# GpSimd's two-operand tensor work moved to VectorE in a two-layer graph kernel

## The reference

```python
def conv(x, a, eps, W, b):            # layer 0, run for x and for x2 with the same adj
    ax = a @ x
    h = ax + (1 + eps) * ax
    for i in range(3):
        h = relu(h @ W[i].T + b[i])
    return h
merged = concat(conv(x, adj, eps1, W1, b1), conv(x2, adj, eps2, W2, b2)) @ Wm.T + bm
x = layernorm(x + merged)
A = adj + eye(4096); deg = A.sum(1); d = where(deg > 0, deg ** -0.5, 0)   # layer 1
x = layernorm(x + ((d[:, None] * A * d[None, :]) @ x) @ W.T + b)
```

## Time and profile before

| | |
|---|---|
| median of 3 runs | 649.18 us (649.15 to 649.63) |
| span of the profiled execution | 647.4 us |
| PE busy | 601.5 us, 93% |
| PEld busy | 485.3 us, 75% |
| DVE busy | 562.9 us, 87% |
| ACT busy | 364.9 us, 56% |
| POOL busy | 272.1 us, 42% |
| HBM read and written | 139.14 MB, 2.10 MB; 218 GB/s over the span |

### The profile page before, as it was taken

How to read it: one execution, slowest core, us unless ns; L and a number is a source line. 1 busy time by engine, 2 the same in 40 slices (tenths; PEclk the granted TensorE clock), 3 DMA queues, 4 the chain that set the end, 5 groups by cost and what they waited for, 6 DMA issues and landing times.

```text
span 647.4 us, 8346 instructions
## 1 busy us (share of the span) xinstructions
PE 601.5 (93%) x2692; PEld 485.3 (75%) x2692; DVE 562.9 (87%) x564; ACT 364.9 (56%) x441; POOL 272.1 (42%) x167
## 2 busy tenths in 40 slices
PE   5949999899999999999999999899989999999984
PEld 4738888678888878888878887557757878878863
DVE  5939998997999998899899799974799988988974
ACT  5514536562353773353675244175786787787772
POOL 0553606780340591160384159960465042340171
PEclk9969999999999999999999999999999999999998
DMA  8943753425536435336534473576588989999800
GB/s 298 413 177 121 269 195 131 175 91 190 189 137 240 149 130 194 130 130 230 183 141 159 162 292 125 199 281 237 196 296 328 359 338 402 344 353 376 320 33 34
DMA packets 21287, 141.54 MB, mean 219 GB/s; under 512 B 2320, under 2 KB 2832, under 8 KB 5008
## 3 DMA queue, kind: packets, MB, share of 16 engines
q1 hardware_dynamic: 20544, 139.15, 58.0%
q10 hardware_dynamic: 720, 2.10, 0.8%
HBM read 139.14 MB, written 2.10 MB: 218 GB/s over the span
## 4 chain that ended last, share of the span: by engine, by line
PE 27%; POOL 24%; issue 22%; DVE 21%; ACT 5%; DMA 1%; POOLq 0%; DVEq 0%; SPq 0%; ACTq 0%
PE ps L332 19%; DVE alo L625 13%; POOL hlo L774 6%; PE pd L350 3%; ACT ahi L482 3%; POOL rstd L790 3%; DVE rowsum L636 2%; POOL x1lo L860 2%; PE pd L362 2%; DVE rowsum L640 2%; POOL xb L780 2%; POOL xb L783 2%; POOL x1lo L822 2%; POOL yt L815 1%; POOL vareps L788 1%
## 5 line engine op out<-in xcount | busy, mean ns | idle before, releaser
L625 DVE TENSOR_TENSOR alo<-raw,ahi 128x1024 fp32r<-128x1024 f32 x255 | 356.0, 1414 | 61.3 <-ACT ahi L482 60.0
L482 ACT ACTIVATE ahi<-raw 128x1024 fp32r<-128x1024 f32 x255 | 267.6, 1059 | 248.1 <-PE ps L332 231.1
L332 PE MATMUL ps<-ahi,x1hi 128*128 128x512 f32 x504 | 163.7, 401 | 34.5 <-DVE alo L625 13.5
L332 PE MATMUL ps<-ahi,x2s 128*128 128x512 f32 x512 | 159.9, 391 | 0.0
L332 PE MATMUL ps<-alo,x1hi 128*128 128x512 f32 x504 | 158.9, 392 | 0.0
L332 PE MATMUL ps<-ahi,x1lo 128*128 128x512 f32 x504 | 158.7, 391 | 0.0
L332 PEld LDWEIGHTS ps<-ahi,x1hi 128*128 128x128 f32 x504 | 92.1, 189 | 66.4 <-issue 26.1
L332 PEld LDWEIGHTS ps<-ahi,x2s 128*128 128x128 f32 x512 | 97.0, 189 | 20.5
L332 PEld LDWEIGHTS ps<-ahi,x1lo 128*128 128x128 f32 x504 | 95.2, 189 | 20.3
L332 PEld LDWEIGHTS ps<-alo,x1hi 128*128 128x128 f32 x504 | 95.2, 189 | 19.9
L774 POOL TENSOR_TENSOR hlo<-h,hhi 128x512 fp32r<-128x512 f32 x36 | 79.2, 2233 | 68.8 <-ACT hhi L487 68.8
(11 more groups left out here) (66 smaller groups left out, 367.1 us busy)
## 6 DMA issues: line engine op xcount, KB each, us to landing
raw<-a_t SPq DMA_DIRECT2D x124, 1024.0 KB, 4.8
raw<-a_t SPq DMA_DIRECT2D x7, 512.0 KB, 8.8
xn<-x SPq DMA_DIRECT2D x3, 1024.0 KB, 8.6
out<-outn ACTq DMA_DIRECT2D x3, 512.0 KB, 5.4
par<-params SPq DMA_DIRECT2D x1, 708.0 KB, 14.2
xn<-x SPq DMA_DIRECT2D x2, 256.0 KB, 4.6
raw<-a_t SPq DMA_DIRECT2D x2, 256.0 KB, 5.1
xn<-x SPq DMA_DIRECT2D x1, 512.0 KB, 8.2
```

Of the source, the lines that this page charges most:

```text
L332: mm = pe.matmul(ps[bank][:, :], block_of(w, n), a[c], start=(n == 0 and k == 0), stop=(n == JB - 1 and k == 2))
L482: act.activation(ahi[:, n % SPLIT, :], raw_tile(layer, n), ACT.Copy).then_inc(hi_ready, 1)
L625: dve.tensor_tensor(alo[:, n % SPLIT, :], raw_tile(layer, n), as_f32(ahi[:, n % SPLIT, :]), ALU.subtract).then_inc(lo_ready, 1)
```

## The change

All of GpSimd's tensor work but the two powers (degrees to the -0.5, variance to the -0.5) goes to VectorE. It is written into VectorE's lists at fixed blocks:

- x pieces 3, 4, 5 are split at blocks 7, 12, 20 of the first quarter; `wlo` between the first and second quarter.
- `hlo` is split at blocks 3, 4 (two tiles each), 7 and 9 (four each) of the next quarter; the base at `DVE_BASE` and the block after.
- the variance plus epsilon stands behind the aggregation, the shift (now one instruction) two or three blocks later, behind a wait for GpSimd's power.
- y of quarters 0 to 2 is made at blocks 12, 20, 28 of the last layer-0 quarter and split two blocks later, that of quarter 3 at blocks 22 and 24 of the first layer-1 quarter. ACT rounds every y, at the block between, in one piece of 1024 (before: GpSimd for six of eight halves). TensorE waits for y once in 8 blocks, before once in 4. `xn` plus the bias is made in place, right behind each split.
- the identity goes into diagonal block n three blocks ahead (`AHEAD`).
- the normalisation of a layer-1 quarter starts on ACT at block 22, before 23.
- more quarters are written out in place of hardware loops on ACT and DVE.

```diff
-ACT_ROUND_Y = (23, 26)
+DVE_BASE = (10, 7)
+DVE_SHIFT = tuple(k + 2 for k in DVE_AGGREGATE)
+DVE_MAKE_Y = (KB + 4, 2 * KB + 4, 3 * KB + 4, 22)
+ACT_ROUND_Y = tuple(k + 1 for k in DVE_MAKE_Y)
+DVE_SPLIT_Y = tuple(k + 2 for k in DVE_MAKE_Y)
+AHEAD = 3
-ACT_NORM2 = DVE_AGGREGATE2 + 6
+DVE_SHIFT2 = DVE_AGGREGATE2 + 3
+ACT_NORM2 = DVE_SHIFT2 + 2
...
+            def round_y(g):                                   # ACT
+                act.wait_ge(yt_ready, g + 1)
+                act.wait_ge(block_used, (QUARTERS - 1) * JB + KB * (g + 1))
+                act.activation(x1hi[:, g, :], yt[:, :, :].rearrange("p k d -> p (k d)"),
+                               ACT.Copy).then_inc(yhi_ready, 1)
...
+            def split_h(q, l, m):                             # all from here: DVE
+                wait(dve, hhi_ready, q * (LAYERS * M) + (M * l + m + 1))
+                dve.tensor_tensor(hlo[:, m, :], h[:, m, :], as_f32(hhi[:, m, :]),
+                                  ALU.subtract).then_inc(hlo_ready, 1)
+            def variances(done, r=slice(0, KB)):
+                wait(dve, stats_ready, done)
+                dve.tensor_scalar(vareps[:, r], mv[:, r, 1], LN_EPS, None, ALU.add).then_inc(var_ready, 1)
+            def shifts(done, r=slice(0, KB)):
+                wait(dve, rstd_ready, done)
+                dve.scalar_tensor_tensor(out=nshift[:, r], in0=mv[:, r, 0], scalar=-1.0, in1=rstd[:, r],
+                                         op0=ALU.mult, op1=ALU.mult).then_inc(norm_ready, 1)
+            def mlp_step(q, n, plan):
+                if plan == 0:
+                    if n in (ACT_EVACUATE + 1, ACT_EVACUATE + 2):
+                        for m in range(CH):
+                            split_h(q, 0, CH * (n - ACT_EVACUATE - 1) + m)
+                    if n in ACT_RELU[0] and ACT_RELU[0][n] < LAYERS - 1:
+                        for m in range(M):
+                            split_h(q, ACT_RELU[0][n] + 1, m)
+                if n == DVE_BASE[plan]:
+                    residual_base(q)
+                if n == DVE_BASE[plan] + 1:
+                    residual_bias(q)
...
+                    variances(q + 1)
+                if n == DVE_SHIFT[plan]:
+                    shifts(q + 1)
+                    degree_factors(q)
+            def split_y(g):
+                dve.wait_ge(yhi_ready, g + 1)
+                dve.tensor_tensor(quarter(x1lo, g), yt[:, :, :], as_f32(quarter(x1hi, g)),
+                                  ALU.subtract).then_inc(y_ready, 1)
+                dve.tensor_tensor(quarter(xn, g), quarter(xn, g), bias_rows(BO_AT), ALU.add).then_inc(base_ready, 1)
+            def add_identity(q, n):
+                wait_raw1(dve, q, n)
+                k = n % KB
+                square = raw_tile(1, n)[:, k * P:(k + 1) * P]
+                dve.tensor_tensor(square, square, identity[:, :], ALU.add).then_inc(identity_added, 1)
...
             def layer1_quarter(q, before):
                 for n in range(JB):
...
+                        y_step(n, (QUARTERS - 1,))
                     else:
                         finish_step(before, n)
+                    if (n + AHEAD) // KB == q:
+                        add_identity(q, n + AHEAD)
...
+            with pool.Fori(0, QUARTERS) as q:                 # GpSimd keeps this
+                degree_power(q)
+                norm_power(q + 1)
+            for q in range(QUARTERS - 1):
+                norm_power(q + QUARTERS + 1)
```

More of the change, by code:

```diff
@@ L223, in identities, with bias_rows, quarter @@
         def identities(q, n):
+            return q * KB + min(max(n - q * KB + 1, 0), KB)
+        def bias_rows(at):
+            return par[:, at:at + P].rearrange("p (o d) -> p o d", o=1).to_broadcast([P, KB, P])
+        def quarter(t, q):
             if isinstance(q, int):
[L226 to L233, removed]
+                return t[:, q, :].rearrange("p (k d) -> p k d", d=P)
+            return t[:, bass.ds(q, 1), :].rearrange("p o (k d) -> p (o k) d", d=P)
         block = ctx.enter_context(nc.Block())
@@ L614, in split_a @@
             def split_a(q, layer, n):
-                if layer == 0 and n == 0 and isinstance(q, int):
+                if layer == 0 and n == 0 and isinstance(q, int) and q == 0:
                     for c in range(CH):
@@ L654, in statistics_taken @@
             def statistics_taken(done):
-                wait(dve, stats_step, done * KB)
+                wait(dve, stats_step, done)
             def aggregate(blocks=range(KB), last=None):
@@ L757, in _ @@
         def _(pool):
-            def quarter(t, q):
-                if isinstance(q, int):
-                    return t[:, q, :].rearrange("p (k d) -> p k d", d=P)
-                return t[:, bass.ds(q, 1), :].rearrange("p o (k d) -> p (o k) d", d=P)
-            steps = [0]
-            def bias_rows(at):
-                return par[:, at:at + P].rearrange("p (o d) -> p o d", o=1).to_broadcast([P, KB, P])
-            def split_h(q):
-                for i in range(LAYERS * M):
-                    wait(pool, hhi_ready, q * (LAYERS * M) + (i + 1))
-                    m = i % M
-                    pool.tensor_tensor(hlo[:, m, :], h[:, m, :], as_f32(hhi[:, m, :]),
-                                       ALU.subtract).then_inc(hlo_ready, 1)
@@ L840, in prepare_layer1, with degree_power @@
-            def prepare_layer1(q):
-                wait(pool, z_ready, q + QUARTERS)
-                dq = dall[:, q, :] if isinstance(q, int) else dall[:, bass.ds(q, 1), :].rearrange("p o k -> p (o k)")
-                pool.tensor_copy(dcur[:, :], dq).then_inc(xb_step, 1)
-                pool.tensor_tensor(xb[:, :, :], quarter(xn, q), bias_rows(BO_AT), ALU.add).then_inc(xb_ready, 1)
+            def degree_power(q):
+                wait(pool, deg_ready, q * 2 + 2)
+                pool.tensor_tensor(degpow[:, :], degc[:, :], halves[:, :], ALU.pow).then_inc(degpow_ready, 1)
@@ L848, in _, with norm_power @@
+            def norm_power(done, r=slice(0, KB)):
+                wait(pool, var_ready, done)
+                pool.tensor_tensor(rstd[:, r], vareps[:, r], halves[:, r], ALU.pow).then_inc(rstd_ready, 1)
             pool.memset(ones[:, :], 1.0).then_inc(const_ready, 1)
             pool.memset(halves[:, :], -0.5).then_inc(const_ready, 1)
-            pool.memset(epsilons[:, :], LN_EPS).then_inc(const_ready, 1)
-            pool.memset(minus[:, :], -1.0).then_inc(const_ready, 1)
             pool.memset(identity[:, :], 0.0).then_inc(const_step, 1)
```

218 lines of the change are left out of this document (82 added, 136 removed).

## The result

The changed kernel took **618.22 us** (median of four runs, 617.99 to 619.22), the kernel before 649.33 in the same comparison. The ratio is 0.9521 (95% interval 0.9507 to 0.9534), so 4.8% faster. The forecast was 618.3. The span of its profiled execution is 617.4; before it was 647.4.

A forecast was written before the change was run, and what follows sets the result against it. TensorE was taken as the bound, delayed by GpSimd's work and its slowing of DVE; gains 11.6 + 13.5 + 2.2 + 0.6 + 3.0 = 30.9 us take the span 647.4 to 616.5, plus 1.8 gives 618.3, range 615 to 622.

The forecast's parts named there:

- Prices: DVE start-to-start costs: 1.13 us for 1024 columns, about 0.60 for 512, about 0.21 for 128; broadcast operands taken at 1.13.
- First quarter: Layer-0 quarter 0: TensorE's 9.3 us idle before block 8 and 2.3 of slow matmuls go; gain 11.6 us.
- The margin at block 8: First quarter: DVE has x piece 3 and block 8's alo ready 1 us before TensorE finishes block 7.
- Layer-0 quarters: Layer-0 quarters 1 to 3: 101.0 us each without waits, DVE's load 87 or 98 fitting under that; gain 13.5 us.
- Layer 1, quarter 0: From block 8 on, 7.2 us of waits are exchanged for 5.0, mostly around block 24's y chain; gain 2.2 us.
- Quarters 1 and 2: Layer 1: present waits of 3.8 us exchanged for 3.2 as DVE lacks room for eight identities; gain 0.6 us.
- Quarter 3 and the end: Layer 1: gain 3.0 us up to the last four blocks; the end between 0.1 faster and 0.3 slower, taken as 0.
- (a): Rival, layer 1: DVE becomes the bound, 8.7 us more, 627; sign: quarters pass 49 us; chance 0.18.
- (b): Rival, layer 1: GpSimd's power gets nothing until DVE stops to wait; 3 us more, 621.3; chance 0.10.
- (c): Rival, first quarter: the split of x still comes late, TensorE idles and cools again; up to 622.6 us; chance 0.06.
- (d): Rival: DVE's 2.32 us instructions come from ACT or TensorE, not GpSimd; the kernel gets slower, 682 us; chance 0.03.
- (e): Rival, layer 1: its waits are overcounted since the lead also recovers between them; 4 us less, 614; chance 0.11.

The follow-up runs named there:

- the undoing run: The changed kernel with x pieces 3 to 5 split by GpSimd again, as before the change: 629.96 us, ratio 0.9695 against the kernel before.
- the run with the memsets: The changed kernel plus 48 GpSimd memsets of 128x512 into an unread scratch tile, from block 18 of the second layer-0 quarter: 618.18 us.
- The experiments on base and y: The changed kernel with quarter 3's layer-1 bias add at block 30, not 24: 617.36 us; with its y also in two halves: 616.84 us.
- Spreading the normalisation: ACT's normalisation at one tile per block over eight blocks, against the kernel combining identities on GpSimd, halved y, late bias add (614.06 us): 613.22 us.
- the subtractions that nobody needs: The changed kernel plus 24 GpSimd subtractions of 128x512 into an unread scratch tile, from block 18 of the second layer-0 quarter: 634.01 us.
- the copies: The changed kernel plus 24 one-input GpSimd copies of 128x512 into an unread scratch tile, from block 18 of the second layer-0 quarter: 619.09 us.

## Why the prediction was right

**Prices.** 1.13 start to start for 1024 columns held (27.51, 28.65, 29.79 above), and a broadcast operand costs nothing more: y at 1214 ns. Identity adds are 0.20 apart (0.21 forecast). `alo` has the mean 1218 ns (1.22 forecast) and its longest is 1251.

**First quarter.** Forecast 11.6, measured 10.7 in the profiled execution and 11.7 in the undoing run. The difference is in the first 14 us: TensorE's matmuls came 0.43 apart until 13.85 us in this execution, until 11.59 in the one of before, and 0.23 apart afterwards. 0.43 is also their distance behind the wait at block 8 of before, where the granted clock is 0.52 of full speed (41 to 46 us), so it is the 1.2 GHz level. It fits that this execution's own time, 619.22, stands 1.0 above the median: the other three have spans of 616.2 to 616.6, where 616.5 was the forecast. The margin at block 8 was 1.7 in this execution and not 1: `alo` was ready at 31.0, TensorE asked at 32.7. But 1.0 of it is TensorE's slow start; in the run with the memsets, where the clock rose at 11.5, `alo` was ready at 30.7 and TensorE asked at 31.47, so the margin is 0.7.

**Layer-0 quarters.** Forecast 101.0 each, measured 100.83. (In the load of DVE, 64 x 1.13 is 72.3 and not 72.6; the 87 stands.) Of the 14.0 of gain 13.5 were forecast. That over half lay in quarter 3 is right too (109.55 to 100.83, with 0.4 of another boundary in it).

**Layer 1, quarter 0.** Forecast a gain of 2.2, measured 2.2. From block 8 on the quarter took 37.8 us for the 32.7 of its blocks, so 5.1 were lost where 5.0 were forecast. The large waits came where they were placed. DVE's and TensorE's rows:

```profile
446.87 1.22 DVE L739 TENSOR_TENSOR yt<-xn,dall 128x1024 f32<-128x1024 f32 x1
...
451.31 1.22 DVE L744 TENSOR_TENSOR x1lo<-yt,x1hi 128x1024 fp32r<-128x1024 f32 x1
...
449.37 0.70 PE L332 MATMUL ps<-ahi,x1hi 128*128 128x512 f32 x2 [0.65 <-DVE alo L625]
452.58 0.72 PE L332 MATMUL ps<-ahi,x1hi 128*128 128x512 f32 x2 [1.60 <-DVE x1lo L744]
454.94 0.70 PE L332 MATMUL ps<-ahi,x1hi 128*128 128x512 f32 x2 [0.70 <-DVE alo L625]
```

Behind the statistics TensorE idled 0.27 at block 15, and with the slower blocks 15 to 18 it lost 0.8 (0.8 forecast). The one of ACT's normalisation came at block 23 with 0.65 (0.4 forecast at block 22; 1.4 late less a lead of 1.3 is in fact 0.1, so the 0.4 wasn't what its terms give). Block 24 waited 1.6 (2.5), block 25 0.70 (0.9). The chain through y measures 446.87 to 452.5, 5.6 us; 5.2 and the hand-overs of 0.4 were the forecast. Block 24 idled less, as the lateness of blocks 22 and 23 had shifted it already. These idle times sum to 3.2; the other 1.9 of the 5.1 lie in blocks beside them that took 0.1 to 0.3 more than 1.36 without an idle time in brackets. The experiments on base and y show that these are the waits that cost.

**Quarters 1 and 2.** Forecast 0.6, measured 0.5: the sum of two opposite things, as described, and the experiment with the identities on GpSimd shows the first of them at 1.4 in quarter 1. In quarter 2 I had 1.4 late; the experiment gives back 0.5 only, so the other waits there, ACT's normalisation among them, are larger than I had them and the identities' smaller. Spreading the normalisation took a further 0.4 and 0.6 from these two quarters. One sign didn't come as forecast: in quarter 1 no idle time with `alo` as releaser stands in the waits. The first matmuls of its blocks 13 and 14:

```profile
484.63 0.70 PE L332 MATMUL ps<-ahi,x1hi 128*128 128x512 f32 x2
...
486.15 0.70 PE L332 MATMUL ps<-ahi,x1hi 128*128 128x512 f32 x2
```

They are 1.52 apart and not 1.36, as are the next two: TensorE went at the pace of DVE's blocks with statistics, forecast at 1.53. The loss is the one that was forecast; it shows as slower blocks.

**Quarter 3 and the end.** 2.9 against 3.0. The end lost 0.4 where I took 0 out of -0.3 to 0.1, just outside: the last blocks wait for `alo`, as before, and for the power. With the identities on GpSimd this last stretch took 16.7 (after 17.4, before 17.0), so its loss hangs on where the identities are, which the forecast had only in the blocks ahead of it.

**The rivals.** (a) DVE as the bound of layer 1: quarters 1 and 2 took 47.57 and 47.15, under its 49. (b) The power shut out: DVE's `nshift` waited for it three times, 0.4 at most. The one wait over 1 us for `rstd` is that of `outn` at the very end, 1.1, where before has 1.4. The power does take 2.42 in the mean beside a busy DVE, but was not held until DVE stopped, as the split of x was, and no `alo` beside it was longer for it (1251 ns at most). Where it took 2.54 to 2.57, it had arrived 0.25 into an `alo`, and its 1.64 undisturbed and the 0.9 that were left of that `alo` make the sum. Why no later instruction of DVE grew by it is not settled. (c) No wait for x at block 8. (d) DVE's long instructions weren't GpSimd's doing: refuted by `alo`'s mean, and by the subtractions that nobody needs, which bring the 2.3 back. (e) Waits of layer 1 overcounted: the sum of its gains is 5.6 of 5.8.

**One reading was wrong.** The forecast says that the 2.32 of DVE in the earlier trace rows shows both engines at about half speed, and that the Trainium skill's rule disagrees with it. The runs show turns of whole instructions. The 2.32 is a DVE instruction that was held for the whole of one of GpSimd. The Trainium skill, SBUF — State Buffer, Who interferes with whom, calls the ports that DVE and GpSimd share an exclusive lock, and exempts GpSimd work that only writes; with that the copies (1.55 apart), the memsets (DVE at 1.22) and `nshift` at 1.25 agree. The sum didn't suffer, since it rests on rows; but whoever believes in half speed would put a short DVE instruction beside GpSimd's wide ones and expect it to cost 0.3.

The size of the deviations, up to 0.9 per stage with both signs, says that the agreement to 0.1 us in the total is partly luck.

## What to carry to other kernels

Work on GpSimd that reads SBUF isn't free because its engine is idle. Where DVE works with two SBUF operands beside it, each GpSimd instruction that reads costs DVE nearly its whole length, even when nobody needs its product, and that price is to be set against what DVE would need itself: 1.10 against 0.60 for 128x512. The exceptions are where DVE waits anyway or has room (the identity adds in layer 1), where it has a lead (the copies), and work that only writes; the power of eight columns lengthened nothing either. And a GpSimd result with a due time shouldn't be asked for while DVE runs without a gap.

## What the runs showed of the hardware

- A GpSimd instruction that arrives while DVE runs two-operand instructions back to back can get nothing until DVE's first gap: 15.15, 50.99 and 12.54 us for instructions of 2.33, 1.3 and 0.46. Others, at 124.90 in before and 161.44 beside the subtractions, had their turn at once, and from a first turn on the two alternate, DVE's gaps or not. What decides is open. Which of the two happens made the difference between TensorE idle for 8.8 us and DVE slowed by two.
- Small DVE instructions pay the same turn: beside the subtractions `gain` of two columns, which reads one tensor only, took 1.25 us (0.16 undisturbed), `nshift` of eight 1.25. They matter where they stand in a chain at the end of a quarter.
- TensorE's matmuls came 0.43 us apart (the lower level) until 11.6 and 11.5 us in two executions and until 13.9 and 13.3 in two others. Block 8 began at 31.47 with 11.5 and at 32.68 and 32.54 with the later two, which is about 1 us of the time from run to run.
